# The two versions of TensorE's attention loop change places in the program of an AdaLN block

## The chip, the cores and the metric

The kernel runs on one core of one Trainium2 chip. The metric is the device time of one execution, in microseconds (us). TensorE (PE in the rows; its weight loads stand as PEld, its sequencer as PEq or PEldq) does the matrix products, VectorE (DVE) and ScalarE (ACT) move and transform data, GpSimd (POOL) does elementwise work, and SyncE (SP) issues nearly all of the DMA transfers. Each engine runs its own straight list of instructions, and they meet only at semaphores.

## What is computed

Eight batches of 512 tokens by 1024 features go through a block with two modulated halves. Cut to what matters:

```
mod = (silu(c) @ wmod)                       # six rows of 1024 a batch: sa, ca, ga, sb, cb, gb
h   = layernorm(x) * (1 + ca) + sa
attn = einsum('ds,td->st', w1, w2) * sparse_mask     # 1024 x 1024, non-zero in a band only
x   = x + ga * gelu(einsum('bds,st->bdt', h, attn) + b2)
h   = layernorm(x) * (1 + cb) + sb
P   = h @ U1;  H = P @ V1 + b1;  gate, up = H[:2752], H[2752:]
x   = x + gb * ((silu(gate) * up) @ U2 @ V2 + b2)
```

All arithmetic is float32. A product is made of three TensorE passes over a high and a low part of each operand.

## The kernel before

The work has three stages. **Start** (0 to about 131 us): the weight product `attn` is formed in a band of columns round the diagonal, masked and split into `attn_hi` and `attn_lo`; the modulation rows are formed one chunk of `wmod` at a time; batch 0 goes through its attention. **Attention loop** (to about 265 us): batches 1 to 7. **Low-rank loops** (from about 267 us to the end): first `P` for all batches, with `turn(t, k)` and `p_product(b, k)`, then the two big products for all batches.

The mask is data. If it has a non-zero outside of the band, the kernel must also work on the far parts of `attn`. VectorE counts those entries, GpSimd reduces the count over partitions into `dense_flag`, and TensorE, ScalarE and VectorE each read the flag into a register, `dense`. ScalarE (line 990) and VectorE (line 1284) have one small `If(dense != 0)` each, whose body is 20 operations on ScalarE and 40 on VectorE. TensorE has the whole attention part of its program twice: `first_batch(whole)` and `attention(b, whole)` for seven batches, once with `whole` false (the banded version) and once with `whole` true (the one for any mask). Each stands in an `If` of its own. With this reference's mask `dense` is 0, so the banded version is the one that runs. An `If` whose condition doesn't hold is a compare-and-branch over its body; one whose condition holds falls into the body.

What TensorE does round the two places that matter, with the lines of the kernel before:

- Ahead of the two `If`s: the eight rounds of the band product (line 563), with the flag's load into `dense` before the last round (line 560), then `mod_product(0)` (line 582, tile `wm_first`).
- `first_batch` begins with `turn(0, 0)` and `turn(0, 1)` (line 608, transposes of the normalized tile `nrm`), which wait until VectorE has masked all eight blocks (`masked_ready`, line 1265), then `mod_product(1)` (line 582, tile `wm_sb`, whose DMA it waits for), then `mod_turn(0)` (line 594). Its transposed rows feed VectorE's `table`, which ScalarE's first `h_hi` (line 1017) and VectorE's first `h_lo` (line 1360) need, and these TensorE's next steps.
- The last thing in the attention loop is `y(7, 7)` (lines 721 and 707). Just before it stands `turn(8, 3)` (line 608).
- The first things of the low-rank loop are `turn(8, 4)` (line 608), `p_product(0, 0)` (lines 545 to 547) and `beta2_turn` (line 664), a tiny transpose that waits for `beta2_row_ready`. VectorE gives that in `beta2_rows` (line 1348), which stands in its list behind `stats2(7, 0)` (line 1238), the bias row (line 1458) and `lo(8, 4)` (line 1360). `stats2(7, 0)` needs a sum that GpSimd makes (line 1586), behind `rstd_and_shift(9)` (lines 1565 to 1571) and a gate product (line 1583).

The order on every engine is the order in which the code is written; nothing is scheduled by a planner.

Of the kernel before, what the change touches and what calls it, by code (L numbers as in the profile page):

```python
# [18 lines left out]
def adaln_block(nc, x, w1, w2t, b2, mask, u1, v1, u2, v2, b1_main, b1_tail, b2f, ct, wmod, out):  # L19
    NB, TOK, D = x.shape  # L20
# [39 lines left out]
    with ExitStack() as ctx:  # L60
# [481 lines left out]
        def _(pe):  # L542
# [7 lines left out]
            def attn_product(acc, s, a, e):  # L550
                for k in range(FB):
                    last = nc.tensor.matmul(acc, w1_sb[:, k, s * P:(s + 1) * P], w2t_sb[:, k, a:e],
                                            start=(k == 0), stop=(k == FB - 1))
                return last

            for k in range(FB):
                pe.wait_ge(w_in[k], 32)
                if k == FB - 1:
                    pe.wait_ge(flag_known, 1)
                    dense = nc.tensor.value_load(dense_flag[0:1, 0:1].bitcast(I32))  # L560
# [7 lines left out]
            def mod_product(q):  # L568
                pe.wait_ge(wm_in[WM_PLACE[q]], 16 * len(before(q)) + 16)
                if q < 2:  # L570
                    pe.wait_ge(masked_ready, q + 1)
                elif q < 4:
                    pe.wait_ge(mod_read, q - 1)
                elif q < 6:
                    pe.wait_ge(lo_ready, FB - 5 + q)
                elif q == 6:
                    pe.wait_ge(ga_first, 2)
                else:
                    pe.wait_ge(mod_read, q)
                for k in range(FB):  # L580
                    j = k % 4
                    last = nc.tensor.matmul(bank[32 * j:32 * j + 32, mod_bank(q), :], c_pad[:, k, :],  # L582
                                            wm_chunk(q)[:, k, :], start=(k < 4), stop=(k >= 4),
                                            skip_group_check=True)
                last.then_inc(mod_mm, 1)
# [4 lines left out]
            def mod_turn(q):  # L590
                pe.wait_ge(mod_rows_ready, q + 1)
                for j in range(4):
                    cols = slice(j * P, (j + 1) * P)
                    last = nc.tensor.transpose(bank[:, mod_bank(q), cols], mod_rows[:, q % 2, cols], ident[:])
                last.then_inc(mod_turned, 1)

            def turn(t, k):
                i = t * FB + k
                if k % 4 == 0:
                    pe.wait_ge(n_ready, t * 8 + k + 4)  # L600
                if turn_before(i) is not None:
                    pe.wait_ge(lo_ready, turn_before(i) + 1)
                elif turn_bank(i) == 6:
                    pe.wait_ge(ga_first, 1)
                if t == 1 and k < 2:
                    pe.wait_ge(mod_read, 5 + k)
                for n in range(TT):
                    last = nc.tensor.transpose(bank[:, turn_bank(i), n * P:(n + 1) * P],  # L608
                                               nrm[:, n, k * P:(k + 1) * P], ident[:])
                last.then_inc(turned, 1)  # L610
# [11 lines left out]
            def beta_first_half():  # L622
                pe.wait_ge(const_in, 32)
                pe.wait_ge(sh_lo_ready, 1)
                pe.wait_ge(attn_lo_ready, FB)
                pe.wait_ge(mod_read, 3)
                for part in near[0][:-1]:
                    attn_shift(*part, part == near[0][0], False)
                bias_rows(0)

            def beta_product(h, whole):
                if h == 0:
                    pe.wait_ge(sh_lo_ready, 2)
                else:
                    pe.wait_ge(mod_read, 4)
                    for part in near[1][:-1]:
                        attn_shift(*part, part == near[1][0], False)
                    bias_rows(1)
                if whole:
                    if h == 0:  # L640
                        pe.wait_ge(dn_lo, len(off_band))
                    for part in far[h]:
                        attn_shift(*part, False, False)
                attn_shift(*near[h][-1], False, True).then_inc(beta_mm, 1)
# [51 lines left out]
            def y_end(b, u, whole):  # L696
                n, h = u % TT, u // TT
                if whole:
                    pe.wait_ge(lo_ready, b * FB + FB)
                    if b == 0:  # L700
                        pe.wait_ge(dn_lo, len(off_band))
                    for part in far[h]:
                        y_part(b, u, part, False)
                if b == 0 and n == 0:
                    pe.wait_ge(pick_made, 3)
                    pe.wait_ge(beta_lo_ready, h + 1)
                nc.tensor.matmul(bank[:, n, :], pick[:, b:b + 1].to_broadcast([P, P]),  # L707
                                 beta[:, h * HALF:(h + 1) * HALF], start=False, stop=True,
                                 skip_group_check=True).then_inc(y_done, 1)
# [29 lines left out]
            def first_parts(at):  # L739
                for u in range(TT):  # L740
                    y_near(0, u, at, at + 1)

            def first_batch(whole):
                pe.wait_ge(masked_ready, FB)
                if whole:
                    for n, (s, a, e) in enumerate(off_band):
                        if n >= 2:
                            pe.wait_ge(dn_masked, n - 1)
                        attn_product(bank[:, n % 2, 0:e - a], s, a, e).then_inc(dn_mm, 1)
                    pe.wait_ge(dn_masked, len(off_band))  # L750
                turn(0, 0)
                turn(0, 1)
                mod_product(1)
                mod_turn(0)
                turn(0, 2)
                first_parts(0)
                mod_turn(1)
                turn(0, 3)
                first_parts(1)
                turn(0, 4)  # L760
                first_parts(2)
                turn(0, 5)
                first_parts(3)
                mod_product(2)
                mod_product(3)
                turn(0, 6)
                mod_turn(2)
                turn(0, 7)
                first_parts(4)
                mod_turn(3)  # L770
                beta_first_half()
                beta_product(0, whole)
                mod_product(4)
                for u in range(TT):
                    y_end(0, u, whole)
                mod_turn(4)
                beta_product(1, whole)
                mod_product(5)
                y(0, 4, whole)
                mod_turn(5)  # L780
                y(0, 5, whole)
                pe.wait_ge(mod_placed, 6)
                gate_turn(6, ga_turned)
                turn(1, 0)
                turn(1, 1)
                first_gates()
                y(0, 6, whole)
                turn(1, 2)
                y(0, 7, whole)
                turn(1, 3)  # L790

            def attention(b, whole):
                q = 5 + b
                turn(b, 4)
                turn(b, 5)
                y_near(b, 0, 0, 4)
                turn(b, 6)
                y_near(b, 0, 4)
                turn(b, 7)
                y_end(b, 0, whole)  # L800
                y(b, 1, whole)
                if b == NB - 1:
                    pe.wait_ge(mod_placed, NCHUNK)
                    gate_turn(7, gb_turned)
                y(b, 2, whole)
                if q < NCHUNK:
                    mod_product(q)
                y(b, 3, whole)
                turn(b + 1, 0)
                y(b, 4, whole)  # L810
                if q < NCHUNK:
                    mod_turn(q)
                turn(b + 1, 1)
                y(b, 5, whole)
                turn(b + 1, 2)
                y(b, 6, whole)
                if b == NB - 1:
                    beta2_product()
                turn(b + 1, 3)
                y(b, 7, whole)  # L820

            with nc.tensor.If(dense == 0):
                first_batch(False)
                for b in range(1, NB):
                    attention(b, False)
            with nc.tensor.If(dense != 0):
                first_batch(True)
                for b in range(1, NB):
                    attention(b, True)

            for b in range(NB):
                t = NB + b
# [872 lines left out]
```

## Time and profile before

| | us |
|---|---|
| median of 3 runs | 1193.31 |
| lowest and highest of them | 1191.06, 1196.17 |
| the profiled execution, its own time | 1192.87 |
| span of the profiled execution | 1191.1 |
| TensorE's granted clock, mean | 0.99 |

The span is the time between the first and the last instruction that the profile records; the execution's own time has 1.8 us more round it. All places below are in microseconds from the span's start. The chain of work that ended last is followed back from the last instruction to what released it each time, and so tells which delays can reach the end. An idle time marked "issue" is one for which the profile shows no other engine or transfer that it waited for.

### The profile page before, as it was taken

To read this page: it belongs to the slowest core of one execution; us is meant where nothing else is said; L and a number is where in the kernel's file an instruction comes from. 1 tells how busy PE (TensorE), PEld (TensorE's weight loads), DVE (VectorE), ACT (ScalarE), POOL (GpSimd) and SP (SyncE) were. 2 spreads that over 40 slices of the span, in tenths; PEclk is the share of its full clock that TensorE was granted. 3 is DMA by queue.
4 is the path that set the end of the run, shared out by engine and by line. 5 is a ranking of instruction groups with operands and counts; after the bars stand their busy time and mean duration, and the time that the engine had idled before them with its cause. 6 is when DMAs were issued, how large, how long until landed. Compare 5 with 4: busy or idle time off the path is not lost.

```text
span 1191.1 us, 15387 instructions
## 1 busy us (share of the span) xinstructions
PE 1149.5 (97%) x5882; PEld 952.4 (80%) x5882; DVE 586.1 (49%) x940; ACT 490.4 (41%) x789; POOL 390.4 (33%) x339
## 2 busy tenths in 40 slices
PE   5798899997999999999999999999999999999998
PEld 5577798886888788888888888888888888888886
DVE  3456687774665334444444444443444434444343
ACT  2136577675887543224223323322422431332241
POOL 1008899863112657313031130311303113031110
PEclk9899999998999999999999999999999999999999
DMA  9993999847554542421040150132114015013101
GB/s 361 388 336 121 325 335 326 295 153 259 230 220 151 196 128 94 159 88 71 27 151 1 71 177 1 72 93 84 71 31 147 3 69 177 1 71 101 41 1 71
DMA packets 57484, 169.59 MB, mean 142 GB/s; under 512 B 6208, under 2 KB 11072, under 8 KB 55360
## 3 DMA queue, kind: packets, MB, share of 16 engines
q1 hardware_dynamic: 57408, 168.57, 39.5%
q8 instruction: 49, 0.80, 0.3%
q14 instruction: 27, 0.22, 0.1%
HBM read 126.51 MB, written 42.04 MB: 142 GB/s over the span
## 4 chain that ended last, share of the span: by engine, by line
PE 85%; DMA 4%; DVE 3%; POOL 3%; SPq 2%; ACT 1%; issue 1%; DVEq 0%; POOLq 0%; ACTq 0%
PE bank L545 21%; PE bank L546 21%; PE bank L547 21%; PE bank L721 6%; PE bank L608 4%; PE bank L922 2%; PE bank L924 2%; PE bank L929 2%; DMA wm_sb<-in_wmod 2%; POOL g L1583 2%; PE bank L582 1%; SPq L378 1%; PE bank L707 1%; POOL xs L1586 1%; DVE bn L1222 1%
## 5 line engine op out<-in xcount | busy, mean ns | idle before, releaser
L1155 ACT ACTIVATE act<-bank,b_sb 128x512 f32<-128x512 f32 (+1 forms) x176 | 121.3, 690 | 497.3 <-PE bank L547 481.4
L1498 DVE SCALAR_TENSOR_TENSOR act<-bank,b_sb,act 128x512 f32<-128x512 f32 (+1 forms) x176 | 132.1, 750 | 375.6 <-PE bank L547 352.5
L545 PE MATMUL bank<-pt,v_hi 128*128 128x512 f32 x688 | 268.6, 390 | 0.0
L546 PE MATMUL bank<-pt,v_hi 128*128 128x512 f32 x688 | 267.7, 389 | 0.0
L547 PE MATMUL bank<-pt,v_lo 128*128 128x512 f32 x688 | 267.7, 389 | 0.0
L1653 POOL TENSOR_TENSOR x2t<-gbb_bc,x2t 128x512 f32<-128x512 f32 x64 | 86.1, 1367 | 245.4 <-DMA x2t<-x_dram 245.4
L1508 DVE TENSOR_TENSOR act_lo<-act,act_hi 128x512 fp32r<-128x512 f32 (+1 forms) x176 | 161.2, 916 | 0.8
L545 PEld LDWEIGHTS bank<-pt,v_hi 128*128 128x128 f32 x688 | 129.1, 188 | 29.8 <-DVE act L1498 2.6
L547 PEld LDWEIGHTS bank<-pt,v_lo 128*128 128x128 f32 x688 | 129.2, 188 | 27.1
L546 PEld LDWEIGHTS bank<-pt,v_hi 128*128 128x128 f32 x688 | 129.2, 188 | 26.2
L545 PE MATMUL bank<-act_hi,u_hi 128*128 128x512 f32 x336 | 131.0, 390 | 0.8 <-DVE act_lo L1508 0.7
L546 PE MATMUL bank<-act_lo,u_hi 128*128 128x512 f32 x336 | 130.7, 389 | 0.0
L547 PE MATMUL bank<-act_hi,u_lo 128*128 128x512 f32 x336 | 130.7, 389 | 0.0
L1360 DVE SCALAR_TENSOR_TENSOR h_lo<-bank,table,h_hi 128x512 fp32r<-128x512 f32 x128 | 93.7, 741 | 53.8 <-ACT h_hi L1017 53.7
L1643 POOL TENSOR_TENSOR v_lo<-v2g,v_hi 128x512 fp32r<-128x512 f32 x32 | 43.6, 1364 | 233.0 <-ACT v_hi L1173 233.0
L1017 ACT ACTIVATE h_hi<-bank,table 128x512 fp32r<-128x512 f32 x128 | 86.9, 684 | 66.0 <-PE bank L608 61.0
L1166 ACT ACTIVATE act_hi<-act 128x512 fp32r<-128x512 f32 (+1 forms) x176 | 109.8, 624 | 7.0 <-DVE act L1498 6.9
L977 ACT ACTIVATE nrm<-xs,shift,rstd 128x512 f32<-128x512 f32 x128 | 100.4, 809 | 19.4 <-POOL shift L1571 19.2
L721 PE MATMUL bank<-attn_hi,h_hi 128*128 128x198 f32 (+2 forms) x320 | 93.2, 291 | 1.6 <-DVE h_lo L1360 1.5
L608 PE MATMUL bank<-ident,nrm 128*128 128x128 f32 x512 | 78.8, 280 | 15.9 <-DVE h_lo L1360 13.8
L721 PE MATMUL bank<-attn_lo,h_hi 128*128 128x198 f32 (+2 forms) x320 | 91.2, 285 | 0.0
L721 PE MATMUL bank<-attn_hi,h_lo 128*128 128x198 f32 (+2 forms) x320 | 91.2, 285 | 0.0
(134 smaller groups left out, 1675.1 us busy)
## 6 DMA issues: line engine op xcount, KB each, us to landing
xs<-in_x SPq DMA_DIRECT2D x32, 512.0 KB, 5.7
wm_sb<-in_wmod SPq DMA_DIRECT2D x8, 2048.0 KB, 10.0
x_dram<-xs SPq DMA_DIRECT2D x32, 512.0 KB, 5.2
xs<-x_dram SPq DMA_DIRECT2D x32, 512.0 KB, 5.2
x2t<-x_dram SPq DMA_DIRECT2D x32, 512.0 KB, 4.1
out<-x2t SPq DMA_DIRECT2D x31, 512.0 KB, 4.9
pt_dram<-pt_st SPq DMA_DIRECT2D x8, 1024.0 KB, 4.5
pt<-pt_dram SPq DMA_DIRECT2D x8, 1024.0 KB, 5.8
```

What stands on the lines that cost most here:

```text
L545: nc.tensor.matmul(acc, s_hi, m_hi, start=start, stop=False)
L546: nc.tensor.matmul(acc, s_hi, m_lo, start=False, stop=False)
L547: return nc.tensor.matmul(acc, s_lo, m_hi, start=False, stop=stop)
L608: last = nc.tensor.transpose(bank[:, turn_bank(i), n * P:(n + 1) * P], nrm[:, n, k * P:(k + 1) * P], ident[:])
L721: nc.tensor.matmul(acc, moving[:, slot, toks], weight[:, s, a:e], start=start and i == 0, stop=False, skip_group_check=True)
L977: nc.scalar.activation(nrm[:, n, cols], source(t)[:, n, cols], ACT.Identity, scale=rstd[:, t, n:n + 1], bias=shift[:, t, n:n + 1]).then_in ...
L1017: nc.scalar.activation(h_hi[:, i % RING, :], bank[:, turn_bank(i), :], ACT.Copy, scale=table[:, t % NB, col:col + 1]).then_inc(hi_ready, 1)
L1155: nc.scalar.activation(act[0:w, j % 2, :], bank[0:w, j % 2, :], ACT.Silu, bias=b1_sb[0:w, i, 0:1]).then_inc(silu_done, 1)
L1166: nc.scalar.activation(act_hi[0:w, slot, :], act[0:w, j % 2, :], ACT.Copy).then_inc(act_hi_ready, 1)
L1360: nc.vector.scalar_tensor_tensor(h_lo[:, i % RING, :], bank[:, turn_bank(i), :], table[:, t % NB, col:col + 1], h_hi[:, i % RING, :], ALU. ...
L1498: nc.vector.scalar_tensor_tensor(act[0:w, j % 2, :], up, b1_sb[0:w, i, 1:2], act[0:w, j % 2, :], ALU.add, ALU.mult).then_inc(act_done, 1)
L1508: nc.vector.tensor_tensor(act_lo[0:w, slot, :], act[0:w, j % 2, :], act_hi[0:w, slot, :], ALU.subtract).then_inc(act_lo_ready, 1)
```

## The change

The two `If` statements of TensorE's program change places. Nothing inside either version, and nothing on another engine, is different.

```diff
-            with nc.tensor.If(dense == 0):
-                first_batch(False)
-                for b in range(1, NB):
-                    attention(b, False)
-            with nc.tensor.If(dense != 0):
-                first_batch(True)
-                for b in range(1, NB):
-                    attention(b, True)
+            with nc.tensor.If(dense != 0):
+                first_batch(True)
+                for b in range(1, NB):
+                    attention(b, True)
+            with nc.tensor.If(dense == 0):
+                first_batch(False)
+                for b in range(1, NB):
+                    attention(b, False)
```

In the rows of the order a COMPARE_AND_BRANCH is the test of an `If`, "waits" names semaphores, and x7 means seven more of the same. TensorE, the kernel before, at the head of the attention part: what stands behind the first test is the banded version.

```order
L582 MATMUL bank<-wm_first,c_pad 32x512 x7
L822 COMPARE_AND_BRANCH
L608 MATMUL bank<-ident,nrm 128x128 [waits n_ready,masked_ready]
L608 MATMUL bank<-ident,nrm 128x128 x7
L582 MATMUL bank<-wm_sb,c_pad 32x512 [waits masked_ready,wm_in0]
```

The changed kernel at the same place: behind the first test stand 3,581 rows of the version for any mask, which begins like this.

```order
L582 MATMUL bank<-wm_first,c_pad 32x512 x7
L822 COMPARE_AND_BRANCH
L552 MATMUL bank<-w2t_sb,w_sb 128x512 [waits masked_ready]
L552 MATMUL bank<-w2t_sb,w_sb 128x512 x7
L552 MATMUL bank<-w2t_sb,w_sb 128x314 x8
```

Behind those rows the changed kernel has its second test, and then the banded version.

```order
L707 MATMUL bank<-beta,pick 128x512
L822 UNCONDITIONAL_BRANCH
L826 COMPARE_AND_BRANCH
L608 MATMUL bank<-ident,nrm 128x128 [waits n_ready,masked_ready]
L608 MATMUL bank<-ident,nrm 128x128 x7
L582 MATMUL bank<-wm_sb,c_pad 32x512 [waits masked_ready,wm_in0]
```

So the jump over those rows is now made by the first test, ahead of `turn(0, 0)`. At the other end, TensorE of the kernel before has its second test behind the banded version, with the same 3,581 rows behind it.

```order
L721 MATMUL bank<-attn_hi,h_lo 128x198
L707 MATMUL bank<-beta,pick 128x512
L822 UNCONDITIONAL_BRANCH
L826 COMPARE_AND_BRANCH
L552 MATMUL bank<-w2t_sb,w_sb 128x512 [waits masked_ready]
```

In the changed kernel the banded version's last product has the low-rank loop's `turn(8, 4)` right behind it; the branch between them leads to the next instruction.

```order
L721 MATMUL bank<-attn_hi,h_lo 128x198
L707 MATMUL bank<-beta,pick 128x512
L826 UNCONDITIONAL_BRANCH
L608 MATMUL bank<-ident,nrm 128x128 [waits lo_ready,n_ready]
L608 MATMUL bank<-ident,nrm 128x128 x3
L545 MATMUL bank<-h_hi,u_hi 128x512 [waits gelu_done,lo_ready]
```

The jump has moved from the end of the attention part to its head.

## Rows read from the trace of the kernel before

**Rows 1.** Page: each engine's busy time, and the engines' shares of the chain.

```profile
PE 1149.5 (97%) x5882; PEld 952.4 (80%) x5882; DVE 586.1 (49%) x940; ACT 490.4 (41%) x789; POOL 390.4 (33%) x339
...
PE 85%; DMA 4%; DVE 3%; POOL 3%; SPq 2%; ACT 1%; issue 1%; DVEq 0%; POOLq 0%; ACTq 0%
```

**Rows 2.** The four tests, by line: ns min/median/max, first and last start.

```profile
L822 PEldq COMPARE_BRANCH  x1: 84/84/84, 48.9 to 48.9; - x1
...
L826 PEldq COMPARE_BRANCH  x1: 3875/3875/3875, 263.4 to 263.4; - x1
...
L990 ACTq COMPARE_BRANCH  x1: 45/45/45, 51.5 to 51.5; - x1
...
L1284 DVEq COMPARE_BRANCH  x1: 71/71/71, 52.1 to 52.1; - x1
```

**Rows 3.** Timeline of TensorE at the seam: start, us, what, [idle before].

```profile
265.37 0.41 PE L707 MATMUL bank<-beta,pick 128*128 128x512 f32 x1
267.46 0.63 PE L608 MATMUL bank<-ident,nrm 128*128 128x128 f32 x4 [1.68 <-issue]
...
268.62 0.40 PE L545 MATMUL bank<-h_hi,u_hi 128*128 128x512 f32 x1
272.35 0.28 PE L664 MATMUL bank<-ident,pt_st 8*128 8x8 f32 x2 [2.87 <-DVE pt_st L1348]
```

**Rows 4.** Timeline of VectorE at the seam, same columns.

```profile
269.98 0.69 DVE L1238 BATCH_NORM_STATS2 bn<-xs 128x6 f32<-128x512 f32 x1 [3.93 <-POOL xs L1586]
...
271.89 0.40 DVE L1348 COPY pt_st<-bank 8x256 f32<-8x256 f32 x1
```

**Rows 5.** Chain of work, 255 to 300 us: start, us, what.

```profile
263.34 0.45 PE bank L608 x4
263.82 0.70 ACT h_hi L1017
...
265.21 0.08 DVE mv L1229
...
268.66 1.28 POOL xs L1586
...
280.73 6.43 DMA xs<-x_dram
...
289.18 0.66 PE bank L608 x4
```

**Rows 6.** Timeline of TensorE at the start, same columns as rows 3.

```profile
48.84 1.92 PE L582 MATMUL bank<-wm_first,c_pad 128*32 128x512 f32 x16
51.03 1.09 PE L608 MATMUL bank<-ident,nrm 128*128 128x128 f32 x8 [0.27 <-DVE masked L1265]
52.53 1.92 PE L582 MATMUL bank<-wm_sb,c_pad 128*32 128x512 f32 x16 [0.41 <-DMA wm_sb<-in_wmod]
54.39 0.66 PE L594 MATMUL bank<-ident,pt_st 128*128 128x128 f32 x4
```

**Rows 7.** Chain of work from the start to the loop, as in rows 5.

```profile
25.81 26.68 DMA wm_sb<-in_wmod
52.53 1.92 PE bank L582 x16
54.46 0.60 PE bank L594 x4
...
85.22 1.07 POOL rstd L1568
...
130.32 1.12 PE bank L608 x4
```

**Rows 8.** DMA queues of 263.4:269, 48:54 and 33:51: packets, MB, share.

```profile
q8 instruction: 2, 0.03, 2.6%
...
q1 hardware_dynamic: 1150, 2.32, 104.5%
...
q8 instruction: 1, 0.02, 0.4%
```

**Rows 9.** DMA issues over the whole span: KB each, median us to landing.

```profile
b_sb<-in_b SPq DMA_DIRECT2D x1, 4.0 KB, 2.2
...
b_sb<-in_b_tail SPq DMA_DIRECT2D x1, 0.5 KB, 9.1
```

**Rows 10.** Stretches: length, busy of PE, PEld, DVE, ACT, POOL; PEclk, DMA, GB/s.

```profile
126.80:130.14 3.34, 0.63 (x4) 0.42 (x4) 3.34 (x5) 1.18 (x2) 3.26 (x3) 0.99 1.03 387
130.14:133.55 3.41, 3.23 (x15) 3.23 (x16) 3.41 (x12) 0.69 (x1) 2.92 (x5) 0.51 1.04 345
```

## The prediction, made before the changed kernel ran

> **What bounds the kernel now.** I read the page first. TensorE is busy for 97% of the span and has 85% of the chain that ended last [rows 1], so a delay of TensorE mostly reaches the end; but it is not all of the chain, and both edits lie at places where TensorE idles. So for each place the question is whether the chain passes through TensorE there.
>
> Next come the tests themselves. The first one, which isn't taken, took 84 ns at 48.9 us; the second, which jumps over the version for any mask, took 3.875 us at 263.4 us [rows 2]. ScalarE and VectorE also take a jump, over 20 and 40 operations, and pay 45 and 71 ns. So what costs here is not the taking of a jump but the taking of a long one. While TensorE's long jump lasts, the queue that carries instructions moves two packets, 0.03 MB together [rows 8]: code is loaded. That is the jump's price, and the change moves it and doesn't remove it.
>
> Then both places. At the seam TensorE's last product starts at 265.37 and the next thing at 267.46, after 1.68 us idle with "issue" as its reason [rows 3]; the jump ends at 263.4 + 3.875 = 267.3. It began while some 16 products were still queued in the engine, and these hid its first 2.4 us, until 265.8. At the start, the test stands at 48.9, just as the 16 passes of `mod_product(0)` begin; TensorE then waits for VectorE's mask until 51.03, and for a DMA until 52.53 [rows 6].
>
> **The seam, where 1.68 us of stall goes.** Without the jump `turn(8, 4)` starts when `y(7, 7)` ends, 1.68 us earlier, and `p_product(0, 0)` follows. Behind these stands `beta2_turn`, which already waits 2.87 us, until 272.35, for VectorE's copy [rows 3]. What is late next is therefore that copy. It starts at 271.89, behind `stats2` at 269.98, which waited 3.93 us for GpSimd's sum [rows 4]. That sum starts at 268.66 and goes back over VectorE's averages (265.21) and ScalarE's `h_hi` (263.82) to `turn(8, 3)` at 263.34 [rows 5], which stands in TensorE's list ahead of `y(7, 7)` and of the jump. Nothing between 263.34 and 271.89 waits for what TensorE does after the jump: the one thing that VectorE takes from there, `lo(8, 4)`, needs `turn(8, 4)`, which was early enough even with the stall. So `beta2_turn` still starts at 272.35 and its wait grows from 2.87 to 4.55 us. The chain itself doesn't touch TensorE here; it comes back to it at 289.18, after a GpSimd stretch, a store and a load of 6.43 us [rows 5]. Gain on the path: 0. The other bound is the whole 1.68 us, if the copy were not what TensorE waits for; I take 0, as the row with 2.87 us is the next row of the same engine.
>
> **The start, where the jump goes.** No row shows a long jump at 49 us, so its length is bounded from other rows. The nearest is the 3.875 us at 263.4: same engine, same rows jumped over. From below stand the short jumps of 45 and 71 ns and the 84 ns [rows 2]; from above a small transfer of 0.5 KB that took 9.1 us where one of 4 KB takes 2.2 us on idle queues [rows 9], 6.9 us more, which would make 10.8 us. The load matters since the data queue q1 fills all 16 DMA engines from 48 to 54 us (a share of 104.5% [rows 8]), while between 263.4 and 269 next to nothing but code moves. Against a high price: one code packet falls into the equally full stretch from 33 to 51 us, and it took 0.4% of 16 engines times 18 us, 1.2 us; the two at the seam took 2.6% of 16 times 5.6 us, 1.2 us each [rows 8]. The packet itself isn't slowed by the load. I take 3.875 us.
>
> The sum: the jump starts at 48.9 and ends at 52.78. At the seam the first product began 0.18 us after the jump's end (267.46 less 267.28). The second test now follows, not taken, 0.08 us. `turn(0, 0)` so starts at 53.04 and not at 51.03, 2.0 us late. Then 8 transposes: the row has 1.09 us for them with the last one's tail, and about 0.86 us until the next may start (it ends at 52.12 and the wait of 0.41 us goes to 52.53). `mod_product(1)` starts at 53.90. Before it started at 52.53, when its DMA had landed; 0.64 us of the delay is thus absorbed by a wait that vanishes, and **1.37 us** is left. The cover of the jump is the 1.92 us of `mod_product(0)`, the wait for the mask and the wait for `wm_sb`: 3.6 us in all between 48.9 and 52.53, and a jump of up to 2.5 us would cost nothing.
>
> Who waits: `mod_turn(0)` at 54.39 [rows 6] follows `mod_product(1)` in order. VectorE's `table`, the first `h_hi` and `h_lo` and all of TensorE's next steps hang on it. On SyncE the fourth `wmod` chunk is issued after `mod_product(1)`, and batch 1's x and all later loads behind it, so those move too. The chain goes from the DMA at 25.81 to `mod_product(1)` at 52.53, and on over TensorE, GpSimd at 85.22 and a load to the loop at 130.32 [rows 7]; everything in it after 52.53 lies behind the delayed step, so no independent branch can absorb the 1.37 us. From 131 us the loop is TensorE's own.
>
> **The Trainium skill weighed.** The long jump took 3.875 us where the untaken test took 84 ns [rows 2]. The Trainium skill, page "Advanced Engine Details and Errata", section Control Flow Timing, gives some 108 ns for a compare-and-branch: the trace roughly agrees for the three cheap ones (45 to 84 ns) and contradicts it for the long one. By that figure the jump at the start would be hidden and the sum would be 0. The Trainium skill, page "Runtime: NRT & Kernel Launch", section Instruction fetch mechanics, says that a taken branch out of the buffered pages waits for a DMA fetch of the target's page; the two code packets of rows 8 agree, and it gives no price.
>
> **Clock.** TensorE's granted clock is 1.2 GHz from 130.14 to 133.55 (0.51), after a stretch in which it was busy for 0.63 of 3.34 us [rows 10]. In the changed kernel TensorE comes back to the loop at 130.32 + 1.37 = 131.7. If the slow stretch stays where it is, less work falls into it and 0.7 us comes back; if another such stretch arises from the new idle time, at most 3.4 / 2 = 1.7 us are lost. I take 0 and keep both for the range.
>
> **Rivals.**
> 1. Forecast: start +1.37, seam 0. The profiled execution would take 1192.87 + 1.37 = 1194.2 us; it lay 0.44 us under the median of the three runs, so the median becomes 1193.31 + 1.37 = 1194.7. Chance 0.62.
> 2. The code load waits its turn in the full DMA engines. This is the rival on the slow side. At half of the extra 6.9 us [rows 9] the jump takes 7.3 us and the delay is 4.8 us: 1198.1, chance 0.13. At all of it the delay is 8.3 us: 1201.6, chance 0.05. For it speaks that the data queue is full just then; against it that the packet's own time didn't grow, and that the 9.1 us transfer stood in the data queue itself, behind others. It costs over 0.5% (6.0 us) from a jump of 8.5 us.
> 3. The seam's 1.68 us does reach the end, and the start costs 1.37: -0.3, 1193.0. For it: TensorE really stands still there and is on the chain for most of the span. Against it: the 2.87 us right behind. Chance 0.10.
> 4. The early jump is no longer than its cover of 2.5 us, since its load can start while TensorE works: no cost, 1193.3. At the seam it had as much work over it and still took 3.875 us. Chance 0.06. The figure of 108 ns in the Trainium skill (page "Advanced Engine Details and Errata") would lead here.
> 5. The change does something else than swap a jump (other waits, another order elsewhere). The order shows the same steps and waits on all engines. With clock stretches falling worse or better by 1.7 us, 1191.6 or 1196.4. Chance 0.04.
>
> **The numbers.** Predicted 1194.7. About 0.5% is what a measurement of this kernel tells from no change, and the three runs alone spread by 5 us. The range goes from 1191, where rivals 3 and 5 and a lucky clock end, to 1199, over the middle case of rival 2; only its long case is left out. Faster by over 0.5% (under 1187.3) needs something none of these has: 0.02. Slower by over 0.5% (over 1199.3) is rival 2's long case and a little of its middle: 0.07. Within: 0.91.
>
> **What would show it.** In the changed kernel's profile: a long test at 48.9 of 3.9 us and a short one of some 0.1 us right behind; `turn(0, 0)` at 53.0; `mod_product(1)` at 53.9 with no DMA wait ahead; the chain with "issue" or the sequencer there in place of the end of the `wm_sb` load. At the seam no "issue" ahead of `turn(8, 4)`, and a wait of 4.5 us in place of 2.87 at line 664; the start of the big products 1.4 us later. It is wrong if the first test is much longer than 4 us (rival 2), if the wait at line 664 doesn't grow (rival 3), or if `mod_product(1)` still starts at 52.5 (rival 4).

## The result, and the profile of the changed kernel

The changed kernel took 1198.36 us (median of 9 runs, 1196.14 to 1200.39). The kernel before, beside it, took 1195.79 us (9 runs, 1191.06 to 1196.23); its three runs shown above had been on the low side. The ratio is 1.0037, with a 95% interval of 1.0025 to 1.0049: slower by 4.4 us, between 3.0 and 5.9. The two medians lie only 2.6 us apart, because the 9 runs of the kernel before fall into two groups (four up to 1194.05 us, five from 1195.79 us) and its median lies in the upper one; the means lie 3.9 us apart. The forecast had the direction (1.4 us slower) but a third of the size.

The tests come first, as rows 2 did. By source line: duration in ns, then where.

```profile
L822 PEldq COMPARE_BRANCH  x1: 6287/6287/6287, 49.2 to 49.2; - x1
...
L826 PEldq COMPARE_BRANCH  x1: 75/75/75, 55.6 to 55.6; - x1
```

The long jump has moved to the first test, and it takes 6.29 us there in place of the 3.875 us that it took at the seam [rows 2]. TensorE's timeline at the start (start, us, what, idle before in brackets) answers to rows 6:

```profile
49.19 1.92 PE L582 MATMUL bank<-wm_first,c_pad 128*32 128x512 f32 x16
55.80 1.94 PE L608 MATMUL bank<-ident,nrm 128*128 128x128 f32 x8 [4.69 <-issue]
57.66 2.58 PE L582 MATMUL bank<-wm_sb,c_pad 128*32 128x512 f32 x16
60.17 0.65 PE L594 MATMUL bank<-ident,pt_st 128*128 128x128 f32 x4
```

`turn(0, 0)` starts at 55.80 in place of 51.03. Of these 4.77 us, 0.35 us stem from earlier: `mod_product(0)` already starts at 49.19 and not at 48.84, as the weights arrived that much later in this execution. The jump makes the other 4.42 us. `mod_product(1)` no longer waits for its DMA. The chain of work now has the stall in it (start, us, what):

```profile
51.33 4.47 issue
55.80 1.94 PE bank L608 x8
57.73 2.51 PE bank L582 x16
60.24 0.60 PE bank L594 x4
```

At the seam, TensorE's timeline answers to rows 3:

```profile
271.14 0.41 PE L707 MATMUL bank<-beta,pick 128*128 128x512 f32 x1
271.40 0.60 PE L608 MATMUL bank<-ident,nrm 128*128 128x128 f32 x4
...
278.11 0.37 PE L664 MATMUL bank<-ident,pt_st 8*128 8x8 f32 x2 [4.73 <-DVE pt_st L1348]
```

No stall stands ahead of `turn(8, 4)` any more, and the wait at line 664 has grown from 2.87 to 4.73 us. The delay against the kernel before is 5.8 us at `y(7, 7)`'s last product (265.37 to 271.14), 3.9 us at `turn(8, 4)` (267.46 to 271.40), and 5.76 us again at line 664 (272.35 to 278.11). The seam gives 1.8 us and takes all of it back in the next wait. VectorE's timeline there has the copy and what holds it up, as in rows 4:

```profile
275.73 0.69 DVE L1238 BATCH_NORM_STATS2 bn<-xs 128x6 f32<-128x512 f32 x1 [3.91 <-POOL xs L1586]
...
277.66 0.40 DVE L1348 COPY pt_st<-bank 8x256 f32<-8x256 f32 x1
```

Between `turn(8, 3)` and this copy lie 8.7 us (268.95 to 277.66), and 8.55 before (263.34 to 271.89). The chain that leads to the copy takes as long as it did, whatever TensorE does after its last product.

### The profile page after: what moved, and what is told of

Same layout as the page of the kernel before. It is cut to its first block, busy times and chain, and to the rows that moved or that the text cites. A ratio compares the mean times of both kernels' runs of the same rounds, so it can differ in the third digit from the quotient of the medians.

```text
span 1196.0 us, 15387 instructions
## 1 busy us (share of the span) xinstructions
PE 1151.6 (96%) x5882; PEld 954.2 (80%) x5882; DVE 588.3 (49%) x940; ACT 490.4 (41%) x789; POOL 390.5 (33%) x339
## 4 chain that ended last, share of the span: by engine, by line
PE 85%; DMA 4%; DVE 3%; POOL 3%; SPq 2%; issue 1%; ACT 1%; DVEq 0%; POOLq 0%; ACTq 0%
PE bank L545 21%; PE bank L547 21%; PE bank L546 21%; PE bank L721 6%; PE bank L608 4%; PE bank L922 2%; PE bank L929 2%; PE bank L924 2%; POOL g L1583 1%; DMA w2t_sb<-in_w2t 1%; PE bank L582 1%; SPq L378 1%; PE bank L707 1%; DMA nrm<-in_wmod 1%; POOL xs L1586 1%
## 5 line engine op out<-in xcount | busy, mean ns | idle before, releaser
L1583 POOL TENSOR_TENSOR g<-g,ga_bc 128x512 f32<-128x512 f32 x64 | 84.6, 1324 | 20.3 <-ACT g L1026 11.3
```

Of the source, the lines that this page charges most:

```text
L1583: nc.gpsimd.tensor_tensor(g[:, n, :], g[:, n, :], ga_bc[:, cols], ALU.mult).then_inc(g_ready, 1)
```

## The experiments

Three explanations of the 6.29 us were open: the code's load waits behind data in full DMA engines; the length belongs to the place in the code, or to being the first long jump; or it is a draw of the moment. Beside them stood the forecast's other claim, that the seam is free.

**No jump at all.**

```diff
-            with nc.tensor.If(dense == 0):
-                first_batch(False)
-                for b in range(1, NB):
-                    attention(b, False)
-            with nc.tensor.If(dense != 0):
-                ...
+            first_batch(False)
+            for b in range(1, NB):
+                attention(b, False)
```

> Leaves out TensorE's version for any mask and both of its tests, so that nothing is jumped over (this reference's mask is banded, so the work that runs is the same). If the stall at the seam is hidden by the wait for VectorE's copy, as forecast, this takes as long as the kernel before, within 1 us, and TensorE's wait at line 664 (its line here) is about 4.5 us in place of 2.87. If the seam's 1.68 us had been on the path, it is 1.7 us faster than before. Either way it is about 4.5 us faster than the changed kernel if the early jump is its whole loss.

Measured: 1193.73 us (12 runs) beside 1195.12 for the kernel before (23 runs), ratio 0.9991 (0.9980 to 1.0001). TensorE's waits (us in total, times, longest):

```profile
PE bank L664 <- DVE pt_st L1343: 4.7, 1, 4.7
```

The wait has grown from 2.87 to 4.7 us with the stall gone. The time alone leaves anything between 2.4 us faster and nothing open, so the whole of 1.7 us would fit it; it is the row that shows where the 1.8 us went, in this kernel and in the changed one.

**A jump at both places.** The changed kernel with one more `If(dense != 0)`, of the same body, behind the banded version.

```diff
             with nc.tensor.If(dense == 0):
                 first_batch(False)
                 for b in range(1, NB):
                     attention(b, False)
+            with nc.tensor.If(dense != 0):
+                first_batch(True)
+                for b in range(1, NB):
+                    attention(b, True)
```

> The changed kernel with a second, never used copy of the version for any mask behind the banded one, so that there is a long jump at the start and one at the seam. If the seam is free: as slow as the changed kernel (about +4.4 us on before), with both long tests in the profile and a wait of about 3 us at line 664. If the seam's stall counts: 1.7 us slower than the changed kernel, about +6 us on before.

Measured: 1198.74 us (12 runs), ratio 1.0030 (1.0017 to 1.0042) to the same 23 runs, 3.6 us slower than before and so no slower than the changed kernel. All three tests, and the two waits of TensorE:

```profile
L822 PEldq COMPARE_BRANCH  x1: 6222/6222/6222, 49.1 to 49.1; - x1
...
L826 PEldq COMPARE_BRANCH  x1: 78/78/78, 55.4 to 55.4; - x1
...
L830 PEldq COMPARE_BRANCH  x1: 3702/3702/3702, 269.1 to 269.1; - x1
...
PE bank L608 <- issue: 6.1, 2, 4.6
PE bank L664 <- DVE pt_st L1352: 3.1, 1, 3.1
```

One program and one execution has both lengths: 6.22 us at the start, 3.70 at the seam, over the same number of instructions. With the stall at the seam back (6.1 less 4.6 = 1.5 us), the wait behind it is 3.1 us again. So the seam's jump is free, and its length there is not the start's.

**No data while TensorE jumps at the start.** SyncE holds back two of the 2 MB loads, in the changed kernel and, as the control, in the kernel before.

```diff
             wm_load(0)
+            sp.wait_ge(dense_past, 1)
             wm_load(1)
             wm_load(2)
             sp.wait_ge(mod_mm, 2)
```

> The changed kernel with two of the 2 MB wmod loads held back until VectorE has passed its own test (52.3 us), so that no data moves while TensorE jumps at about 49 us. Theory one, the code load waits behind data in full DMA engines: the jump takes 3.9 us, as at the quiet seam, in place of 6.29. Theory two, the jump's length comes from its place in the code or from being the first: it still takes about 6.3 us. The held loads cost some 5 us of their own, so the total tells nothing of the jump.

> The kernel before with the same two loads held back: the control. Its jump at the seam stays at 3.9 us under both theories. In both held kernels the load of wm_sb lands at about 59 us, so that even the early jump is over before mod_product(1) can start: their totals should agree within the clock's scatter (2 us).

The first test of the held changed kernel, and the DMA queues between 46 and 53 us (packets, MB, share of 16 engines; q1 carries the data, q8 the code):

```profile
L823 PEldq COMPARE_BRANCH  x1: 3687/3687/3687, 48.3 to 48.3; - x1
...
q1 hardware_dynamic: 11, 0.02, 3.2%
q8 instruction: 2, 0.03, 2.3%
```

With the data gone the jump takes 3.69 us at the same place in the code. Its place in the code and its being the first long jump are thus ruled out as the cause of the extra length. In the control the seam's jump took 3.82 us.

Both were then timed over six runs.

> The changed kernel with two wmod loads held back to 52.3 us, timed. If the early jump costs only what sticks out of its cover, the swap costs nothing here, since TensorE waits for the late wm_sb load (7.0 us in the look before) after the jump: this and its control agree within 1 us. If the swap has another cost (a worse clock, for one), this stays 1 to 4 us slower than its control.

> The kernel before with the same loads held back, timed: the control. Both held kernels are about 6 us (0.5%) slower than the kernel before, by the late wm_sb load.

Measured: 1202.10 us (6 runs, ratio 1.0060, 1.0043 to 1.0076) for the held changed kernel, 1203.80 us (6 runs, ratio 1.0081, 1.0065 to 1.0097) for the control. Two of the expected numbers were missed: the medians are 1.7 us apart, not within 1 us, and by the ratios the two are 7.2 and 9.7 us slower than the kernel before, not 6. A held change that is 1 to 4 us slower than its control, as a further cost of the swap would make it, is not what was measured; the pair differs the other way, by about 2 us, with overlapping intervals, and nothing is read from that difference. TensorE's timeline of the held changed kernel, in the execution whose test is shown above, has the cover:

```profile
52.28 1.06 PE L609 MATMUL bank<-ident,nrm 128*128 128x128 f32 x8 [2.09 <-issue]
60.32 1.94 PE L583 MATMUL bank<-wm_sb,c_pad 128*32 128x512 f32 x8 [6.97 <-DMA wm_sb<-in_wmod]
```

2.09 us of stall are followed by 6.97 us of waiting for the held load, where the control waits 8.28.

**One load held back.**

```diff
             wm_load(0)
             wm_load(1)
+            sp.wait_ge(attn_mm, FB)
             wm_load(2)
             sp.wait_ge(mod_mm, 2)
```

> The changed kernel with only the third wmod load (2 MB) held back until the band product is done (48.8 us). If what counts is whether data moves at the moment of the jump, and the second load is still under way then, the jump takes 6.2 us as before; if the second load has landed by 49 us without the third beside it, the jump takes 3.7 us, turn(0, 0) starts at 53.0 and mod_product(1) at 53.9, and the whole is 2 to 3 us faster than the changed kernel.

> The kernel before with the same load held back: the second load lands earlier than 52.49 us, mod_product(1) may start at 51.9 in place of 52.53, a gain of 0.6 us at most at that place, lost again if the third load is late for mod_product(2) at about 67 us.

Measured: one run each, 1195.98 and 1195.41 us beside 1194.07 for the kernel before. The first test of the changed one:

```profile
L823 PEldq COMPARE_BRANCH  x1: 5167/5167/5167, 47.8 to 47.8; - x1
```

5.17 us lies between the two lengths, which neither expectation had. The engines are as full as before at the jump (a data share of 104.4% from 47.8 to 50.5 us). When the jump begins, one load less is queued, but SyncE issues that load at 47.91 us, only 0.1 us later. Why the wait is 1.1 us shorter stays open. In the control `mod_product(1)` started at 52.51, so the second load did not land earlier, and the hoped for 0.6 us did not come.

**Data while TensorE jumps at the seam.** The other direction: the kernel before, with two copies of 2 MB to a scratch tensor in HBM added, started just ahead of the seam.

```diff
+                else:
+                    sp.wait_ge(turned, NB * FB + 3)
+                    for i in range(2):
+                        sp.dma_start(junk_dram[i], wmod[:, i * HALF:(i + 1) * HALF]).then_inc(junk_in, 16)
                 x2_store(b, 0)
```

> The kernel before with two added copies of 2 MB each (2 KB pieces of wmod, to a scratch tensor in HBM), started at about 259 us so that they are under way when the jump at the seam is made (263.4 us). Theory one (the code load waits behind data in full DMA engines): that jump grows from 3.9 us to 6.2, as at the start. Theory two (place in the code or first jump): it stays at 3.9. The end moves by less than 3 us, by the stores and loads that the copies delay.

In the second kernel the source is `x[i]`.

> The same with pieces of 4 KB (rows of x) in place of 2 KB. If the code load waits behind a fixed number of pieces per DMA engine, the wait of some 2.4 us doubles and the jump takes about 8.6 us; if it waits for a fixed time or amount of data, or gets a share of the engine, it takes about 6.2 us again; if pieces of this copy are cut to the same size, likewise.

The second test of each, and the DMA queues from 259.5 to 271 us, first of the copy of `wmod`, then of the copy of `x`:

```profile
L834 PEldq COMPARE_BRANCH  x1: 6735/6735/6735, 263.2 to 263.2; - x1
...
DMA packets 1737, 3.55 MB, mean 309 GB/s; under 512 B 16, under 2 KB 16, under 8 KB 1735
...
q1 hardware_dynamic: 1735, 3.52, 99.0%
q8 instruction: 2, 0.03, 1.1%
```

```profile
L834 PEldq COMPARE_BRANCH  x1: 8485/8485/8485, 263.3 to 263.3; - x1
...
DMA packets 82, 4.23 MB, mean 368 GB/s; under 512 B 16, under 2 KB 16, under 8 KB 16
...
q1 hardware_dynamic: 80, 4.19, 107.5%
q8 instruction: 2, 0.03, 1.1%
```

The seam's jump grows from 3.875 to 6.74 us (6.2 had been expected). So the long jump is long where data moves and short where none does, at either place and in either direction, and this cause is shown. Whether the code waits in the DMA engines themselves or for something else that the data fill, such as the memory, these runs don't separate.

The second kernel was meant to have packets of 4 KB, and its rows show that it hadn't: of 80 packets 16 are tiny, and 64 carry 4.19 MB, 65 KB each. So its 8.49 us lie near the 8.6 of the expectation by chance. By the rows' shares a packet of 65 KB occupies its engine for some 3.1 us (107.5% of 16 engines over 11.5 us, by 64) and one of 2 KB for 0.1 us (99.0%, by 1735). The extra of 4.6 us is thus worth one or two of the big packets, and the extra of 2.9 us nearly thirty of the small ones, so it is no fixed number of packets that the code's load waits for. What it does wait for stays open. One reason not to read a rule from these two lengths: in both, a code packet that in the kernel before moved ahead of the jump (one lies between 257 and 263.4 us there) falls behind the jump's start, and the one for the jump's target comes only after it, so part of the extra may be that of a load which was asked for earlier.

These two executions also show how much the seam swallows. With the copy of `wmod`, TensorE's stall there is 4.59 us in place of 1.68, and the chain of work doesn't feel it (GpSimd's sum, then TensorE's return to the chain; 268.66 and 289.18 in rows 5):

```profile
268.39 1.26 POOL xs L1594
...
288.51 0.65 PE bank L616 x4
```

With the copy of `x` the stall is 6.29 us. The totals, 1192.64 and 1190.86 us beside 1194.07, are single runs and add nothing.

**The changed kernel once more.**

> The changed kernel once more, beside the same runs of the kernel before. The jump takes 6.2 to 6.3 us again if its length is steady. By the jump's measured 6.29 us in place of 3.875 and the 1.37 us of the forecast's own sum, the loss is 3.8 us (ratio 1.0032); the interval of the first measurement was 1.0025 to 1.0049.

Measured: 1198.49 us (12 runs) beside 1193.77 (17 runs), ratio 1.0036 (1.0024 to 1.0049).

```profile
L822 PEldq COMPARE_BRANCH  x1: 6207/6207/6207, 48.9 to 48.9; - x1
...
PE bank L664 <- DVE pt_st L1348: 4.7, 1, 4.7
PE bank L608 <- issue: 4.6, 1, 4.6
```

The length is steady: 6.29, 6.22 and 6.21 us in three executions with full engines, and 3.58 to 3.88 us in seven with quiet ones (3.875 before; 3.70 in the kernel with both jumps; the rest in the held kernels and their controls). It is no draw.

## Why the prediction was right or wrong

**The price of the early jump: wrong, and this is the step that failed.** "I take 3.875 us" chose the row of the same engine and the same code over what differs between the two moments, which was named in the same paragraph: a data share of 104.5% against next to none [rows 8]. Measured were 6.29 us, 2.41 more. The argument against a high price was that a code packet takes 1.2 us in full and in empty engines alike. That is nearly true (the packets of the two jumps take 1.4 us in the kernel before and 1.1 us in the changed one) and beside the point, since it is the time of the packet once it moves. What grows is the time until it moves. In the changed kernel the queue of the code has no packet at all in the first 3.7 us of the jump (queues from 49.2 to 52.9 us, then from 52.9 to 53.1 us):

```profile
DMA packets 719, 1.44 MB, mean 389 GB/s; under 512 B 16, under 2 KB 16, under 8 KB 719
...
q1 hardware_dynamic: 719, 1.44, 105.0%
...
q8 instruction: 1, 0.02, 35.2%
```

while in the kernel before its packet stands within the first 1.6 us (263.4 to 265 us), alone, and is the only one of the whole jump (263.4 to 267.3 us):

```profile
q8 instruction: 1, 0.02, 5.6%
...
q8 instruction: 1, 0.02, 2.3%
```

The prediction counted two packets while that jump lasts [rows 8]; the second moves only after the jump's end. With one packet the jump comes apart into three pieces: 1.0 us until the packet starts, 1.4 us for the packet and 1.4 us after it in the kernel before; 3.8, 1.1 and 1.4 us in the changed one. The whole extra is in the first piece.

Rival 2 had this mechanism, with the bounds 7.3 and 10.8 us for the jump and a chance of 0.18 for both; the truth lies between it and the forecast. The bound of 6.9 us from rows 9 was far too high for a load on a queue of its own, but a value between the ends, and not the lower row, was what rows 8 asked for.

**The sum behind the price: right.** It says that what a jump takes beyond 2.5 us is lost, so 6.29 us cost 3.8 us. Against the kernel before, the profile after has TensorE's steps 4.25 us late at 66 us (61.64 to 65.90), of which 0.35 are older: 3.9 us. Both timed ratios, 1.0037 and 1.0036, hold 3.8 us (1.0032) in their intervals. One term is missing from the sum: `mod_product(5)` now waits for its load, which SyncE issues later, as all loads behind `mod_product(1)`.

```profile
PE bank L582 <- DMA nrm<-in_wmod: 0.6, 1, 0.6
```

This wait stands in all three executions with the full early jump (the changed kernel twice, and the kernel with both jumps) and neither in the kernel before nor in the one without a jump. Of the 0.6 us, 0.2 to 0.3 are left by 120 us: the same product of TensorE starts there at 120.04 in the kernel before and at 124.43, 123.99 and 124.52 in these three, of which 0.3, 0.1 and 0.2 are older. That makes a loss of 3.9 to 4.3 us up to this place.

**The seam at no gain: right, nearly to the number.** 4.55 us were forecast for the wait at line 664, 4.73, 4.7 and 4.7 us measured where no jump stands ahead, and 2.87 to 3.1 where one does. The chain through `turn(8, 3)`, VectorE's averages, GpSimd and the copy is the one that was read in rows 3 to 5. Rival 3 is gone.

**The clock: not settled.** The slow stretches (1.2 GHz) of the changed kernel, as in rows 10 (length; busy of PE, PEld, DVE, ACT, POOL; PEclk; DMA; GB/s):

```profile
55.63:59.04 3.41, 3.24 (x16) 1.96 (x20) 0.00 (x0) 0.00 (x0) 0.00 (x0) 0.50 0.13 45
59.04:106.83 47.79, 40.65 (x336) 30.40 (x329) 29.43 (x68) 21.39 (x34) 10.16 (x13) 1.00 0.73 266
134.14:140.96 6.82, 5.73 (x28) 5.74 (x28) 6.72 (x16) 1.83 (x3) 4.39 (x7) 0.50 1.00 350
277.49:284.32 6.83, 6.21 (x20) 5.21 (x21) 2.54 (x5) 2.73 (x4) 4.52 (x4) 0.50 0.53 215
```

The first now falls on `mod_product(1)`, which takes 2.58 us for 1.92, but it stands in place of the one that lay 3 us later, and the delay shrinks from 5.8 to 4.25 us once TensorE is past it. The one at 134 us is twice as long as its answer in rows 10. In the second execution of the changed kernel it wasn't, and that execution's span was 1193.0 us. Nor is all of the scatter the clock's. The load of x that stands on the chain ahead of the loop took 7.43 us in the kernel before, 7.99 in the first execution of the changed kernel and 6.45 in the second. By these things the first execution is 4.9 us late at the loop's start (130.32 to 135.23) and 5.0 us from 300 us on (300.07 to 305.06), and the second 3.0 and 1.9 us. One pair of profiles is therefore no measure of this loss; the timed ratios are. The mean granted clock was 0.986 over the changed kernel's 9 runs and 0.987 over its 12, and 0.989 over the 17 runs of the kernel before beside the latter; whether the swap itself makes a slow stretch more likely can't be told from that.

**The level: low, and the range hit by luck.** The forecast started from 1193.31 us, the median of three runs with a spread of 5 us; over 9 runs the same kernel had 1195.79. Of the 3.7 us between the forecast 1194.7 and the measured 1198.36, these 2.5 us have nothing to do with the change. What the change itself adds was missed by 1.2 us as the medians have it and by 3.0 us as the ratio has it (4.4 against 1.4), of which 2.4 are the price of the jump. That 1198.36 lies in the stated range of 1191 to 1199 doesn't bear out the forecast's mechanism; the upper end had been set by the middle case of rival 2.

**The 108 ns of the Trainium skill** (page "Advanced Engine Details and Errata", section Control Flow Timing) are of the size of the tests that aren't taken (75 to 84 ns here), lie above the short jumps (45 and 71 ns [rows 2]), and say nothing of a long one. The Trainium skill, page "Runtime: NRT & Kernel Launch", section Instruction fetch mechanics, has the mechanism, a fetch of the target's page by a DMA queue of the sequencer's own, and the runs agree: the code's queue moves a packet inside each long jump. They give it a price: 3.6 to 3.9 us with quiet DMA engines, 5.2 to 6.3 us with the start's data, 6.7 and 8.5 us with the added copies.

## What to carry to other kernels

A branch over a large unused version of a loop costs a few microseconds of the engine's supply of instructions, so put it where the engine waits for something later that doesn't depend on it, as at this seam, which swallowed a jump of 3.9 us, and in the kernel with the copy of `wmod` a stall of 4.6 us, with no delay on the chain of work. Don't put it into the load phase, where it took 6.2 to 6.3 us here: the code's load has to get in between the data. And when a price is moved from one moment of the program to another, ask first which resource it uses and how full that is at either moment; the time of one packet doesn't tell how long it waited.

## What was not expected of the hardware

- A code load on a queue of its own still waits for data that fill the 16 DMA engines: the long jump took 2.4 us more at the start, with a data share of 103 to 105%, and 2.9 and 4.6 us more at the seam with copies added.
- It doesn't wait for the end of the data. In the changed kernel the data share is 103% over the whole jump, 49.2 to 55.5 us, and the code's packet moved at 53.0, in the middle of it.
- A copy within HBM between two contiguous pieces ran in packets of 65 KB, not by the tensors' rows of 4 KB.
